# Sorted edge steps of a graph network: the waits of TensorE rearranged, and the node sums of VectorE moved behind the low half of the activation

## What is computed

```python
for _ in range(4):
    e_in = jnp.concatenate([edge_attr, x[src], x[dst]], axis=-1)
    e_upd = _layernorm(_swish(e_in @ eW1 + eb1) @ eW2 + eb2, eg, ebeta)
    edge_attr = edge_attr + e_upd
    agg = jax.ops.segment_sum(edge_attr, dst, num_segments=N_NODES)
    n_in = jnp.concatenate([x, agg], axis=-1)
    x = x + _layernorm(_swish(n_in @ nW1 + nb1) @ nW2 + nb2, ng, nbeta)
```

## Time and profile before

| | |
|---|---|
| median of 3 runs | 2650.18 us (2649.66 to 2650.37) |
| span of the profiled execution | 3010.4 us |
| PE busy in it | 2519.3 us (84%) |
| DVE busy | 2296.5 us (76%) |
| ACT busy | 1995.8 us (66%) |
| POOL busy | 1569.8 us (52%) |

### The profile page before, as it was taken

How to read it: one execution, slowest core, us unless ns; L and a number is a source line. 1 busy time by engine, 2 the same in 40 slices (tenths; PEclk the granted TensorE clock), 3 DMA queues, 4 the chain that set the end, 5 groups by cost and what they waited for, 6 DMA issues and landing times.

```text
span 3010.4 us, 83926 instructions
## 1 busy us (share of the span) xinstructions
PE 2519.3 (84%) x27990; PEld 1876.1 (62%) x27990; DVE 2296.5 (76%) x6586; ACT 1995.8 (66%) x5343; POOL 1569.8 (52%) x1581
## 2 busy tenths in 40 slices
PE   3699999999858888888876888888885888888885
PEld 1467776677536666666645666666663666666664
DVE  5499999899637787777854787777773688877787
ACT  2478787777437777777635777777753777777774
POOL 0566666664056666666215666666603666666640
PEclk9799999999989999999999999999998999999998
DMA  3556666564256666667445666666734555555540
GB/s 95 158 180 178 185 184 186 177 184 147 93 151 206 209 207 207 207 209 210 129 137 156 209 210 208 206 207 210 209 101 138 161 168 168 168 166 167 167 134 22
DMA packets 380881, 512.91 MB, mean 170 GB/s; under 512 B 57676, under 2 KB 254418, under 8 KB 380440
## 3 DMA queue, kind: packets, MB, share of 16 engines
q1 hardware_dynamic: 305176, 301.81, 32.0%
q0 software_dynamic: 75264, 205.62, 24.0%
HBM read 389.35 MB, written 117.85 MB: 168 GB/s over the span
## 4 chain that ended last, share of the span: by engine, by line
PE 76%; issue 11%; ACT 4%; another core or an unknown queue 4%; DVE 3%; DMA 1%; POOL 0%; DVEq 0%; ACTq 0%; SPq 0%; POOLq 0%
PE psum L1647 17%; PE psum L1615 16%; PE psum L1603 13%; PE psum L1678 6%; PE psum L1595 6%; PE psum L1629 4%; PE psum L1384 3%; PE psum L2081 3%; PE psum L1642 2%; PE psum L2120 2%; PE psum L2094 1%; PE psum L1659 1%; ACT arena L1765 1%; ACT psum L1744 1%
## 5 line engine op out<-in xcount | busy, mean ns | idle before, releaser
L1572 POOL DMA_INDIRECT arena<-node_tables,idx_all x1568 | 1567.2, 999 | 1345.2 <-remote 528.1
L1843 DVE SCALAR_TENSOR_TENSOR arena<-psum,arena 128x1024 f16<-128x1024 f32 x392 | 479.6, 1223 | 520.6 <-issue 370.9
L1743 ACT ACTIVATE arena<-psum 128x1024 f16<-128x1024 f32 x392 | 401.1, 1023 | 576.4 <-PE psum L1615 443.9
L1647 PE MATMUL psum<-w_hi,arena 128*128 128x128 f16 x6272 | 604.1, 219 | 37.5 <-ACT psum L1752 21.9
L1603 PE MATMUL psum<-ident,arena 128*128 128x128 f16 x6272 | 481.4, 220 | 165.9 <-issue 160.5
L1647 PE MATMUL psum<-w_lo,arena 128*128 128x128 f16 x3136 | 553.1, 219 | 3.8 <-issue 3.1
L1647 PEld LDWEIGHTS psum<-w_hi,arena 128*128 128x128 f16 x6272 | 498.2, 98 | 75.8 <-ACT psum L1752 40.3
L1603 PEld LDWEIGHTS psum<-ident,arena 128*128 128x128 f16 x6272 | 390.4, 98 | 242.1 <-issue 222.5
L1615 PE MATMUL psum<-arena,w_hi 128*128 128x512 f16 x1568 | 473.3, 384 | 41.3 <-ACT arena L1789 39.8
L1765 ACT ACTIVATE arena<-psum 128x128 f32<-128x128 f32 x1568 | 412.5, 279 | 100.9 <-remote 79.2
L1744 ACT ACTIVATE psum<-psum 128x1024 f32<-128x1024 f32 x392 | 398.9, 1018 | 0.0
(11 more groups left out here) (174 smaller groups left out, 3258.7 us busy)
## 6 DMA issues: line engine op xcount, KB each, us to landing
state<-arena SPq DMA_DIRECT2D x294, 256.0 KB
arena<-state SPq DMA_DIRECT2D x294, 256.0 KB
arena<-node_tables SPq DMA_DIRECT2D x784, 64.0 KB
arena<-matrices SPq DMA_DIRECT2D x294, 128.0 KB
node_tables<-arena SPq DMA_DIRECT2D x100, 256.0 KB, 2.2
arena<-node_tables,idx_all POOLq DMA_INDIRECT x1568
arena<-rel_rows SPq DMA_DIRECT2D x98, 128.0 KB
matrices<-arena SPq DMA_DIRECT2D x98, 128.0 KB
```

The costliest lines, as they stand in the source:

```text
L1572: pool.indirect_dma_start(out=rows[n % R][:, t, :], out_offset=None, in_=p_table, in_offset=bass.IndirectOffsetOnAxis(ap=idx_all[:, n % G1 ...
L1647: x = pe.matmul(ps_v(k2)[:, t * P:(t + 1) * P], h[k2][:, half, t * P:(t + 1) * P], w[:, half, :], start=False, stop=half == 1 and h is hl, ...
L1743: act.activation(hh[k2], ps_h(k2), ACT.Silu).then_inc(S("hh"), 1)
L1843: dve.scalar_tensor_tensor(hl[k2], ps_h(k2), 1.0, hh[k2], ALU.mult, ALU.subtract).then_inc(S("hl"), 1)
```

## The change

Three things are done. Some waits of PE are dropped where an earlier wait implies them, with the two fences. Others are moved ahead to an instruction that had none. And in DVE's slot, `add_window(n-8)` is put behind `low(n)`; only the read of its window's place stays at the head. The wait for `added`, which stood ahead of `node_sums(n-7)`, now stands in `output(n-1)` ahead of the last quarter of its matmuls, for all but the first and last groups of a step.

```diff
@@ encode
-                    pe.wait_ge(Z(f"at{n % R}"), 16 * self.ring(n))
+                    if n < LAG + 2:
+                        pe.wait_ge(Z(f"at{n % R}"), 16 * self.ring(n))
@@ hidden
-                    if s:
-                        pe.wait_ge(S(f"oh{k}"), 16 * self.ring(n))
-                    else:
+                    if s == 0 and n < 2:
                         pe.wait_ge(Z("oht"), n + 1)
                     pe.wait_ge(S(f"q{k}"), 32 * self.ring(n))
-                    if n >= 2:
-                        pe.wait_ge(S("hl"), n - 1)
-                    fence(pe)
...
                     for half in range(2):
                         cols = slice(half * D, (half + 1) * D)
+                        if half and s == 0 and n >= 3:
+                            pe.wait_ge(S("seed"), n - 2)
@@ turn
-                    if n > G1:
-                        pe.wait_ge(S("eT"), n - G1)
                     for p in range(2):
+                        if p:
+                            pe.wait_ge(S(f"oh{n % R}"), 16 * self.ring(n))
@@ output
-                    if s == 0 and n >= 2:
+                    if s == 0 and n == last:
                         pe.wait_ge(S("seed"), n - 1)
-                    else:
+                    if s or n < 2:
...
                     pe.wait_ge(S("hl"), n + 1)
                     for t in range(TPG):
+                        if t == 1 and s == 0 and n + 2 <= last:
+                            pe.wait_ge(Z("oht"), n + 3)
+                        if t == TPG - 1 and n - 6 > first:
+                            pe.wait_ge(S("added"), n - 6)
@@ turn_back
                     for t in range(TPG):
+                        if t == 2 and n + LAG + 2 < G1:
+                            pe.wait_ge(Z(f"at{(n + LAG + 2) % R}"), 16 * self.ring(n + LAG + 2))
@@ node_sums
                     pe.wait_ge(S("el"), n + 1)
-                    if n:
+                    if n == first and n or n + 6 > last:
                         pe.wait_ge(S("added"), n)
-                    if s == 0:
-                        pe.wait_ge(Z("oh"), n + 1)
-                    fence(pe)
@@ DVE, slot
-                    add_window(n - LAG - 4, window(n - LAG - 4))
+                    w = window(n - LAG - 4)
                     matrices_of(n + 2)
                     first_low(n + 1)
                     low(n)
+                    add_window(n - LAG - 4, w)
```

## The result

The changed kernel takes 3515.27 us (median of 4 runs, 3509.30 to 3517.35), the kernel before 2649.92 us beside it (4 runs, 2648.91 to 2650.37). The ratio is 1.3263, 95% interval 1.3247 to 1.3279: 865 us slower. The prediction was 3560 us, between 3450 and 3700.

The account below looks back on a forecast made before the run. PE's own matmul spacing was taken to bound the kernel before, a PE-ACT-DVE loop the changed one: 506 (rest) + 3 x 700 (later steps) + 893 (step 0) + 64 (clock) = 3563, rounded to 3560 us, range 3450 to 3700.

Parts of the forecast that it names:

- The mechanism: output(n-1) waits for an addition now behind low(n), which needs hidden(n): a loop through PE, ACT and DVE per group.
- The loop of the later steps: Steps 1 to 3: 7.3 us a group, bounds 7.2 to 7.6, for 91 of 98 groups; 700 us a step.
- Step 0: First step's edge loop: seven groups at 6.7 us and 91 at 9.3, 893 us, plus 64 us for the clock.
- the clock: PE's granted clock falls to half in step 0, 1.7 us a fall, two in five groups: 64 us.
- The upper bound: Clock term in step 0: one fall in every group, another 91 us on top of the sum.
- The rest: Set-up, node stages and end, outside the four edge loops: 506 us.
- The reading of the long profile: Runs without a profile have few of its holes in PE; the changed kernel's profile comes within some 2% of its median.
- PE's own 5.07 us: PE's work per group without holes, taken to bound later steps before the change: 497 us a loop, 2655 us in all.
- The dropped waits: PE's dropped waits and fences: taken as no gain; by the skill's rule alone a gain of up to 110 us.
- The full clock in step 0: Rival: PE's clock does not fall in step 0, so the sum is 3499 us; chance 0.18.
- Falls in all steps: Rival: the clock falls in the later steps too, 232 us more, 3795 us; chance 0.13.
- The gain: Rival: DVE finishes low(n) before PE reaches output's last quarter, so the change helps: 2540 to about 2620 us; chance 0.02.

Follow-up runs that it names:

- the activation twice: The changed kernel with one more Silu of ACT ahead of the two in the later steps, its output overwritten: 4154.34 us.
- the sum one group further on: DVE adds group n-7's sums, not n-8's, behind low(n): from the changed kernel 2624.70 us, from the kernel before with all waits and fences 2623.29 us.
- the clock kept full: The changed kernel with ten matmuls of zeros ahead of the wait in output, in step 0 only: 3366.66 us.
- the DVE order alone: The kernel before with DVE's addition put behind low(n) and every wait and fence of PE as it was: 3332.21 us.
- the long profiled execution: First profile of the kernel before, the earlier trace, which the prediction read: span 3010.4 us, 360 us above the median.
- the second profile: The kernel before, unchanged but for a comment, profiled once more: span 2648.8 us, 2650.57 us measured.
- The kernels that differ in fences alone, or nearly: The kernel before without its two fences, 2658.52 us; the changed kernel with its wait ahead of node_sums and no fence, 3355.73 us.

## Why the prediction was right, step by step

**The mechanism** is as predicted: the addition behind `low(n)` closes a loop from `hidden` through ACT and DVE back to `output`, once per group, for 91 groups of a step. The waits name it with that count, the activation twice lengthens it, and the sum one group further on opens it.

**The loop of the later steps.** Worked out as 7.2 us, taken as 7.3; it is 7.13 in the timeline, a little below the 7.2 to 7.6 that were named as the sign. The parts: 3.92 us to the wait's end instead of 4.0, then 3.21 us instead of 3.19. The safety of 0.1 us on top was not needed. By the marks of the earlier trace rows, second group's `hidden` to node stage, step 1's loop takes 1889.36 - 1211.12 = 678 us, predicted 700. The loop's 0.17 us, 91 times, is 15 of these 22. Another 5 is a miscount: 870.03 in the earlier trace rows is the second group of step 1, so the loop measured from there has 97 groups (6.36 us each, not 6.29), and the first group is in the rest as well as in the 700.

**Step 0** should take 893 + 64 = 957 us from the first `hidden`; it took 1111.55 - 98.29 = 1013. With the clock kept full it is 866, below the 893 (a group takes 9.09 us, worked out as 9.2 and taken as 9.3). So the loop was well sized, and **the clock is the term that was mis-sized**: 149 us and not 64. The step of the argument that failed is "I take two in five groups": with a wait of 2.6 us in every group the lower clock returned so often, and lasted up to 10.2 us at a stretch, that it holds a third of the loop. A fall costs more than once, too: at half clock the way to the next wait is longer. The upper bound, a fall in each group at 1.7 us (155 us), was the better estimate. The comparison of durations behind it, 1.81 us without a fall and 2.69 with one, was too coarse as well: with the DVE order alone a wait of 1.93 us in step 0 is followed by a fall, and in the changed kernel's later steps 1.87 us never is.

**The rest** was taken as 506 us and is 3507.6 - 1013.3 - 3 x 678.4 = 459 us (the other two loops last as long as step 1's within 0.4 us). The 506 came from the long profiled execution, where a node stage's start and the next step's second group are 870.03 - 755.89 = 114.1 us apart; here it is 1211.12 - 1111.55 = 99.6 us, three times 14.5 us less. These three errors, +56, -65 and -47 us, add to -56: 3563 becomes 3507. That the sum came so near is in part luck: the clock's error hid half of the other two.

**The reading of the long profile.** The prediction took it that the holes ahead of L1603 were not in the other runs. That is right, as the second profile shows, and with it that the changed kernel's span would be near its median (3507.6 and 3515.27). But that PE's own 5.07 us bound the runs of before is wrong, and the sum that seemed to prove it, 2655 against 2650 us, agreed by luck. In the chain of the second profile the second group of step 1 begins here:

```profile
809.05 1.47 PE psum L1615 x6
```

The loop of step 1 takes 1334.66 - 809.05 = 525.6 us and not 497. From the first `hidden`, at 99.48 in the same chain, step 0 takes 610.4 us and not 658, and the rest is 2648.8 - 610.4 - 3 x 525.6 = 462 us and not 506. Three loops taken 86 us too short hid 48 and 44 us too many. PE still waits in the later steps, 62.4 us ahead of L1678 among others. So "little left to take" was wrong as well: the sum one group further on gains 26 us there.

**The dropped waits** were taken as nothing. The kernels that differ in fences alone, or nearly, bear that out: no gain, and 9.5 and 24 us of loss. The passage of the Trainium skill that was weighed (Perfetto Trace Analysis, Identifying Dependency Chains) names the EventSemaphore instructions and gives no cost for them; the gain of up to 110 us was the prediction's own reading of it. 1721 instructions are indeed gone, and the time is not.

**The rivals.** The full clock in step 0 would have given 3499 us, and its kernel gave 3367: of the 132 us between, 85 are the clock's term (149 and not 64), and the others are what the whole sum was too high by, 3563 against 3515. Falls in all steps did not come, but the activation twice shows them 1.02 us away. The gain needed `low(n)` done 1.88 us after the last `hidden` matmul; it is done 3.68 us after (1506.38 - 1502.70). The prediction also read the 297 waits of DVE in the earlier trace rows as waits for the activations, where the row says only "issue"; in the changed kernel the list names ACT, 328 times.

## What to carry to other kernels

When an instruction moves behind another on one in-order engine, or a wait moves forward on another, write down the group numbers around the circle: if they return to the same iteration, the whole way round becomes the length of an iteration, however idle each engine is. Here the cure was to shift the iteration (add group n-7, not n-8) and not the instruction. And where a wait on the loop also idles PE, count the clock with it, as lasting and returning rather than as single falls, and take a second profile where the profiled execution is far from the median.

## What was not expected of the hardware

- PE waits of 1.87 us in a loop of 7.1 us left the clock full in the later steps' groups, but waits of 1.93 us in step 0 with the DVE order alone, in a loop of some 9.6 us, did not (a mean of 0.86). Waits of 2.6 to 2.9 us brought it to half for a third of step 0 and over a quarter of the stretched steps. In step 0 of the changed kernel one wait of 2.68 us left it full and the next, of 2.67 us, did not. So the length of the wait alone does not decide, and what else does was not tried. Ten matmuls of zeros ahead of each wait kept it full and took 149 us off.
- A wait held by the weight load instead of the sequencer was no faster: 3355.73 against 3332.21 us at nearly the same place, and 2658.52 against 2649 us without the fences. Why is open.
- One execution of the kernel before took 3010.4 us and its next profile 2648.8 us. The first has 160.5 us of holes inside the 16 matmuls of L1603, put down to "issue", which the second has not.
